# Distance attention: three square roots taken before the products

## What is computed

```
scores = einsum(q, k) / sqrt(8)
p = softmax(where(maskb, scores, -1e32)) * maskb
cum, tot = cumsum(p), sum(p)
pos = |j - i|
dist_scores = sqrt(clip((tot - cum) * pos, 0))
gamma = -softplus(gammas)              # one for each head
diff = exp(sigmoid(pdiff))             # one for each i, j
total_effect = clip(exp(dist_scores * gamma * diff), 1e-5, 1e5)
scores = softmax(where(maskb, scores * total_effect, -1e32)); row 0 set to 0
out = einsum(scores, v)
```

## Time and profile before

| | us |
|---|---|
| median of three runs | 1319.47 |
| lowest and highest | 1316.46, 1320.29 |
| the profiled execution, device time | 1316.28 |
| its span, first to last instruction | 1314.5 |
| VectorE busy, whole span | 970.5 (74%) |
| TensorE busy, whole span | 893.0 (68%) |
| ScalarE busy, whole span | 635.5 (48%) |
| layer 2, from the first product (L1301) to the last norm's copy (L189) | 88.5 to 289.2 |

### The profile page before, as it was taken

The page is one execution under the profiler, slowest core; times in us unless marked ns, Lnnn a source line. Parts: engine busy times, 40 slices in busy tenths (PEclk is TensorE's granted clock), DMA queues, the critical chain, the costliest instruction groups (busy, mean ns, idle before and its releaser), DMA issues. The chain is left out here.

```text
span 1314.5 us, 18468 instructions
## 1 busy us (share of the span) xinstructions
PE 893.0 (68%) x6150; PEld 587.3 (45%) x6150; DVE 970.5 (74%) x2494; ACT 635.5 (48%) x1392; POOL 244.2 (19%) x369
## 2 busy tenths in 40 slices
PE   5956667645887303154897938899978625999876
PEld 2523333323455103043894523576645314666644
DVE  5898989937665598987456855788868497898832
ACT  4767667631444403155214722787447421666632
POOL 1330000001000000000012211189522022332100
PEclk9975555557998656667898978899979767999978
DMA  6000000002355200010100000000000000000000
GB/s 211 2 1 0 1 1 1 1 1 96 83 105 131 45 0 34 33 67 34 33 2 1 2 1 1 0 1 1 1 1 1 1 0 0 1 1 2 1 1 16
DMA packets 26607, 30.12 MB, mean 23 GB/s; under 512 B 1169, under 2 KB 23057, under 8 KB 25490
## 3 DMA queue, kind: packets, MB, share of 16 engines
q1 hardware_dynamic: 26514, 28.95, 7.9%
HBM read 19.50 MB, written 9.44 MB: 22 GB/s over the span
## 5 line engine op out<-in xcount | busy, mean ns | idle before, releaser
L1957 PEld LDWEIGHTS l2a_b_ps<-l2a_diag,l2a_uT 128*128 128x128 f32 x512 | 66.2, 198 | 27.8 <-issue 15.4
L1957 PE MATMUL l2a_b_ps<-l2a_diag,l2a_uT 128*128 128x128 f32 x512 | 70.6, 283 | 4.8 <-DVE l2a_convh L2168 3.8
L2654 PE MATMUL l1w_mem_ps<-l1a_rows,l1w_post 128*128 128x64 f32 x16 | 4.6, 381 | 96.7 <-DVE l1a_rows L2796 96.7
L2769 DVE MATCH_REPLACE8 l1w_minus<-l1w_low,l1w_minus 128x129 f32<-128x129 f32 (+39 forms) x264 | 64.3, 256 | 0.0
L2682 ACT ACTIVATE l1w_score<-l1w_mix_ps 128x264 f32<-128x264 f32 (+7 forms) x29 | 12.0, 451 | 106.9 <-DVE l1a_rows L2796 91.1
L2763 DVE MAX8 l1w_low<-l1w_minus 128x8 f32<-128x129 f32 (+37 forms) x332 | 59.5, 254 | 0.4
L2644 PE MATMUL l1w_mix_ps<-l1a_rows,l1w_pre 128*128 128x264 f32 (+7 forms) x58 | 29.6, 681 | 42.2 <-DMA l1a_rows<-scores_dram 24.5
L2627 POOL TENSOR_SCALAR_AFFINE_SELECT l1w_score<-l1w_score 128x256 f32<-128x256 f32 x8 | 4.1, 506 | 247.5 <-ACT l1w_score L2682 247.5
L2654 PEld LDWEIGHTS l1w_mem_ps<-l1a_rows,l1w_post 128*128 128x128 f32 x16 | 4.1, 291 | 101.0 <-DVE l1a_rows L2796 99.9
L613 ACT ACTIVATE l3a_l3x_probT<-l3a_l3x_turn_ps 128x512 f32<-128x512 f32 x64 | 38.2, 596 | 22.7 <-PE l3a_l3x_turn_ps L494 22.0
L494 PE MATMUL l3a_l3x_turn_ps<-pack,l3a_l3x_prob 128*128 128x128 f32 x256 | 40.8, 282 | 10.3 <-ACT l3a_l3x_probT L613 5.7
(11 more groups left out here) (577 smaller groups left out, 2784.9 us busy)
## 6 DMA issues: line engine op xcount, KB each, us to landing
scores_dram<-l1p_dots SPq DMA_DIRECT2D x8, 924.0 KB, 7.1
l1a_rows<-scores_dram SPq DMA_DIRECT2D x5, 1056.0 KB, 4.8
l1a_rows<-scores_dram SPq DMA_DIRECT2D x24, 132.0 KB, 3.7
scores_dram<-l1p_dots SPq DMA_DIRECT2D x8, 132.0 KB, 3.8
pack<-in_pack SPq DMA_DIRECT2D x1, 761.5 KB, 9.6
pack<-in_pack SPq DMA_DIRECT2D x2, 321.5 KB, 6.6
pack<-in_pack SPq DMA_DIRECT2D x1, 612.0 KB, 11.6
pack<-in_pack SPq DMA_DIRECT2D x1, 576.0 KB, 10.6
```

Source lines behind the costliest of these rows:

```text
L1957: mm = nc.tensor.matmul(bx_ps(n)[:, j * S:(j + 1) * S], uT[:, c, b, :], diag[:, s % 2, b, :], start=True, stop=True)
L2769: nc.vector.match_replace(out=neg[:, i, 0:keys[i]], in_to_replace=low[:, i, :], in_values=neg[:, i, 0:keys[i]], imm_value=LOWEST).then_inc ...
```

## The change

In `DistanceAttention.scalar`, `root` no longer takes the root of the products: it takes the root of `left` itself, in place, as soon as the scan of that half is done. Two new steps take the root of `grid` for this batch (128 x 128) and of `rate` (128 x 16), in place, and `load_exponential_table` puts an exponential of one element behind them. `effect` now reads the products from `left` and writes `dist`. The order of ScalarE's steps in `rest()` changes as the diff shows: the roots come early, and the copies of the probabilities stand between them and the effects.

In `DistanceAttention.vector`, the products are taken out of `remaining` and become `products`, which writes back into `left`; it waits for the roots of its half, of the grid and of the rate. It stands behind `statistics`. `divide` moves behind `second_scores`. The scan waits until the effect of the batch before has read `left`, and the first step of `rate` until the products of the batch before are done.

```diff
--- before.py
+++ after.py
@@ -905,8 +905,9 @@
         self.rz = sc.sb("rz", [128, H])
         self.sums = sc.sb("sums", [128, HH, S])
         self.o, self.oT = sc.sb("o", [128, D]), sc.sb("oT", [128, D])
-        self.one_root = sc.sb("one_root", [128, 1])
+        self.one_root, self.one_weight = sc.sb("one_root", [128, 1]), sc.sb("one_weight", [128, 1])
         self.table_set = sc.sem("table_set")
+        self.grid_root, self.rate_root = sc.sem("grid_root"), sc.sem("rate_root")
         self.ln = LayerNorm(sc)
         (self.zero_set, self.ones_set, self.restart_set, self.pad_set, self.qk_mm, self.qk_set,
          self.v_mm, self.v_set, self.scores_mm, self.max_set, self.diff_set, self.first_set, self.left_set, self.rate_set, self.product_set, self.root_set, self.effect_set,
@@ -1082,11 +1083,14 @@
         last_mx = self.last_mx
         first = self.first
         dist = self.dist
+        left, rate, grid, distances = self.left, self.rate, self.grid, self.distances
+        left_set, rate_set = self.left_set, self.rate_set
+        grid_root, rate_root = self.grid_root, self.rate_root
         prob = self.prob
         probT = self.probT
         sums = self.sums
         oT = self.oT
-        one_root = self.one_root
+        one_root, one_weight = self.one_root, self.one_weight
         table_set = self.table_set
         ln = self.ln
         ones_set = self.ones_set
@@ -1116,6 +1120,7 @@
         inside = lambda b: 0 <= b < B
         turn = lambda b, half, part: 4 * b + 2 * half + part
         scale = DH ** -0.5
+        W = S + 1
 
         def first_weights(b, half):
             act.wait_ge(diff_set, 2 * b + half + 1)
@@ -1128,12 +1133,24 @@
             nc.scalar.activation(one_root[:], w("bq"), ACT.Sqrt, scale=0.0).then_inc(table_set, 1)
 
         def root(b, half):
+            act.wait_ge(left_set, 2 * b + half + 1)
+            nc.scalar.activation(left[:, half, :, 1:W], left[:, half, :, 1:W], ACT.Sqrt).then_inc(root_set, 1)
+
+        def root_grid(b):
+            act.wait_ge(distances.grid_set, b + 1)
+            nc.scalar.activation(grid[:, b, :], grid[:, b, :], ACT.Sqrt).then_inc(grid_root, 1)
+
+        def root_rate(b):
+            act.wait_ge(rate_set, 3 * b + 3)
+            nc.scalar.activation(rate[:], rate[:], ACT.Sqrt).then_inc(rate_root, 1)
+
+        def load_exponential_table():
+
+            nc.scalar.activation(one_weight[:], w("bq"), ACT.Exp, scale=0.0).then_inc(table_set, 1)
+
+        def effect(b, half):
             act.wait_ge(product_set, 2 * b + half + 1)
-            nc.scalar.activation(dist[:, half, :, :], dist[:, half, :, :], ACT.Sqrt).then_inc(root_set, 1)
-
-        def effect(b, half):
-            act.wait_ge(root_set, 2 * b + half + 1)
-            nc.scalar.activation(dist[:, half, :, :], dist[:, half, :, :], ACT.Exp,
+            nc.scalar.activation(dist[:, half, :, :], left[:, half, :, 1:W], ACT.Exp,
                                  scale=-1.0).then_inc(effect_set, 1)
 
         def exponential(b, half):
@@ -1182,18 +1199,24 @@
                     copy_v(now)
                 if inside(now):
                     load_root_table()
+                    root(now, 0)
                 if inside(now - 1):
                     copy_probT(now - 1, 0, 1)
+                if inside(now):
+                    root(now, 1)
+                    root_grid(now)
+                    root_rate(now)
+                    load_exponential_table()
+                if inside(now - 1):
                     copy_probT(now - 1, 1, 0)
+                if inside(now):
+                    effect(now, 0)
+                if inside(now - 1):
                     copy_probT(now - 1, 1, 1)
                 if inside(now):
-                    root(now, 0)
+                    effect(now, 1)
                 if inside(now - 1):
                     copy_sums(now - 1)
-                if inside(now):
-                    root(now, 1)
-                    effect(now, 0)
-                    effect(now, 1)
                 if inside(now - 2):
                     ln.act_copy(act, nc, cm, nT_ps, now - 2)
                 if now == 0:
@@ -1230,7 +1253,7 @@
         first_set = self.first_set
         left_set = self.left_set
         rate_set = self.rate_set
-        product_set = self.product_set
+        product_set, root_set, grid_root, rate_root = self.product_set, self.root_set, self.grid_root, self.rate_root
         effect_set = self.effect_set
         scaled_set = self.scaled_set
         last_max = self.last_max
@@ -1284,22 +1307,26 @@
         def remaining(b):
             for half in range(2):
                 dve.wait_ge(first_set, 2 * b + half + 1)
+                after(dve, effect_set, 2 * (b - 1) + half + 1)
                 nc.vector.tensor_tensor_scan(flat(left[:, half, :, :])[:, ::-1], flat(restart[:])[:, ::-1],
                                              flat(first[:, half, :, :])[:, ::-1], 0.0,
                                              ALU.mult, ALU.add).then_inc(left_set, 1)
             dve.wait_ge(left_set, 2 * b + 2)
+            after(dve, product_set, 2 * b)
             nc.vector.tensor_scalar(rate[:], left[:, :, :, 0], 1e-18, None, ALU.max).then_inc(rate_set, 1)
             dve.wait_ge(rate_set, 3 * b + 1)
             nc.vector.reciprocal(rate[:], rate[:]).then_inc(rate_set, 1)
             dve.wait_ge(rate_set, 3 * b + 2)
             nc.vector.tensor_tensor(every(rate), every(rate), gamma2[:], ALU.mult).then_inc(rate_set, 1)
-            dve.wait_ge(rate_set, 3 * b + 3)
-            dve.wait_ge(distances.grid_set, b + 1)
+
+        def products(b):
             for half in range(2):
-                after(dve, prob_set, 2 * (b - 1) + half + 1)
+                dve.wait_ge(root_set, 2 * b + half + 1)
+                dve.wait_ge(grid_root, b + 1)
+                dve.wait_ge(rate_root, b + 1)
                 for h in range(HALF):
                     last = nc.vector.scalar_tensor_tensor(
-                        out=dist[:, half, h, :], in0=left[:, half, h, 1:W], scalar=rate[:, half, h:h + 1],
+                        out=left[:, half, h, 1:W], in0=left[:, half, h, 1:W], scalar=rate[:, half, h:h + 1],
                         in1=grid[:, b, :], op0=ALU.mult, op1=ALU.mult)
                 last.then_inc(product_set, 1)
 
@@ -1344,14 +1371,16 @@
                     remaining(now)
                 if inside(now - 2):
                     statistics(now - 2)
+                if inside(now):
+                    products(now)
                 if inside(now + 1) and now:
                     copy_qk(now + 1)
                 if inside(now - 2):
                     ln.dve_scale(dve, nc, cm, now - 2)
+                if inside(now):
+                    second_scores(now)
                 if inside(now - 1):
                     divide(now - 1)
-                if inside(now):
-                    second_scores(now)
 
         return copy_qk, constants, differences, remaining, rest
 
```

## The result

The changed kernel takes 1303.47 us (median of 4, 1302.83 to 1304.40) against 1318.22 (median of 4) for the kernel before on the same chips: ratio 0.9893, 95% interval 0.9877 to 0.9908. That is 12.1 to 16.2 us less.

What follows compares the result with a forecast made beforehand. The prediction took layer 2 to run at VectorE's pace plus a 1.28 us gap per middle batch. Savings of 0.05 + 1.0 + 6.65 + 2.85 = 10.5 us from the 1319.47 median gave 1309.0, range 1304.5 to 1315.

Steps and rivals of the forecast that it cites:

- the effect's wait: VectorE's wait for ScalarE's effect ahead of L1311 in layer 2: 9.7 us over 8 batches, to be gone or under 1.
- A middle batch then takes 22.44 + 0.2 = 22.64: Layer 2, batches 2 to 6: VectorE's work plus a stall, 1.33 us less per batch, 6.65 for five.
- The 0.2: Ahead of the products in a middle batch: 0.1 us stall for the roots and 0.1 for added, already fulfilled waits.
- The 22.44 of VectorE work: Sum of VectorE's steps in a middle batch of layer 2, against 23.97 us with the gap and divide's wait.
- The scale: Whole time: 10.5 us less, set on the median of three runs, 1319.47, giving 1309.0 us.
- Batch 0: First batch of layer 2: early roots win what the later products lose, 0.05 us gained.
- Divide: VectorE's divide moved behind the shifts: 0.85 us less in batch 7, some 0.25 of waiting for TensorE per middle batch.
- TensorE's slack before the second difference: Middle batch: scores of the second half ready at 24.7, VectorE asks at 25.0, so 0.3 us to spare.
- the ring: Loop through scores, turned heads, copy of V, table load, roots and products; the prediction checked single waits in it.
- Rivals 1: ScalarE's table switch costs its 1.28 us twice, products stall 1.4 per middle batch: 1317.2 us in all; chance 0.04.
- rival 2: TensorE becomes the bound, its chain to the next scores 1 us later: 3.5 us lost, 1313; chance 0.09.
- 3: ScalarE's copy (0,1) between the roots is held by TensorE, products wait 4 us: 16 us slower, 1335.5; chance 0.05.

Runs made afterwards that it cites:

- no_small_roots: Changed kernel without the roots of grid and of rate, so it computes another function: 1301.13 us (1 run).
- more_waits: Changed kernel with eight more, long fulfilled waits ahead of the first product of each half: 1310.56 us, ratio 0.9958 against the kernel before.
- divide_back: Changed kernel with divide put ahead of second_scores again: 1318.52 us, ratio 1.0013 against the kernel before.
- no_early_exp: Changed kernel without the early exponential of one element, the table loading just ahead of effect 0: 1303.54 us, ratio 0.9898 against the kernel before.

## Why the prediction missed

By its own steps:

- What bounds the layer, and that the effect's wait goes: right. So were the two table loads for each batch, no drain around them (182.08 starts 0.02 after the rate's root), and the products' start in batch 1 (0.80 later than without the wait, 0.75 forecast). That the second exponentials of batch 7 come at 257.26, with 257.4 forecast, is luck: this execution came to its first scan 1.8 later than the one the forecast was built on, and the layer gave 1.9 more.
- "A middle batch then takes 22.44 + 0.2 = 22.64": this is the step that failed, as a size. It takes 22.29. The 0.2 ("Between 0 and 0.2 I take 0.1, and 0.1 more for the added waits") measured 0.09: statistics and the wait behind it take 182.20 - 181.30 = 0.90, where the sum had 0.81. Root 1 follows its scan by 0.04, and without the two small roots a middle batch is only 0.03 shorter (no_small_roots), so that next to nothing of it is a stall for the roots. more_waits doesn't show that waits in this place are free: eight more cost 0.36 there.
- The 22.44 of VectorE work was 0.24 too much. I had taken rate to the next instruction as 0.21, the step of an instruction that waits for its own engine's last result; statistics doesn't, and follows by 0.11 (181.19 to 181.30), 0.10 less. copy_qk to the norm's scaling is 0.92 (186.41 to 187.33) and not 1.02, another 0.10, and the rest is in hundredths. The 0.11 and the 0.24 are 0.35 for each of five batches, 1.75 of the 1.9 us by which the layer's sum was short.
- The scale, the other term that was mis-sized. I set the sum on the median of three, 1319.47. Later medians of the same kernel are 1316.99 (23 runs), 1317.8 (14), 1317.7 (9) and 1317.3 (9). From 1317.4 the forecast would have been 1306.9, and with the measured 12.4, 1305.0. This is 2 of the 5.5 us of the miss, the layer 1.9; what remains, 1.5, is as much as the changed kernel's own medians differ by, 1303.5 and 1304.9.
- Batch 0: -0.13, not 0.05. The products lie beside GpSimd's last steps there and take 4.63 in place of 4.29.
- Divide: the part of the mechanism that the prediction had wrong. I had it as worth 0.85 in batch 7 and, in a middle batch, the 0.25 that it waits for TensorE. divide_back shows that the early roots give nothing without its move: the layer is 15.0 longer. My own numbers had it (sums turned at r = 18.4, L1311 at 16.7), but I only asked whether divide would be late in its new place, not what its old one would cost. The sum came out near because the change had both parts, which is luck of the order and not a merit of the sum.
- TensorE's slack before the second difference, 0.3 in the prediction, was 0.57 in the trace and 0.2 for the ring. Rivals 1, 2 and 3 did not come; the ring's 0.2 says that rival 2 was close.

## What to carry to other kernels

Where an engine's wait is cut, list for each of its later instructions when its input lands, in the old order as well as in the new: two moves that are each worth nothing can be worth 12 us together. Take the step between two instructions from a row with the same pair and the same wait, since 0.1 us in a step of a loop of five is half a us. Set sums on the stretch that is changed, not on one median of three.

## What the runs showed of the hardware

- Eight fulfilled waits ahead of an instruction cost VectorE 0.35 us behind short steps, 0.06 in batch 1, where it stood idle for another engine, and nothing behind 128x128 products that were running (more_waits).
- A table load does not wait for the semaphore of the activation behind it (no_early_exp), and a switch is 1.28 us of load with 0.01 to 0.02 on each side, in all 16 of the layer, before and after. The Trainium skill's page "ScalarE: Activation LUTs", section "What ACT_TABLE_LOAD costs", adds a drain of about 1380 ns; none of these 16 has room for one.
- The same code takes up to 4.6 us more in layer 1, by TensorE's granted clock in the stretches 20 to 30 and 30 to 40 us. At 1.00 and 1.00 the first scan is at 83.3; at 0.83 and 1.00 at 84.4 to 85.2 (nine traces); at 0.66 and 1.00 at 85.8; at 0.66 or 0.67 and 0.82 or 0.83 at 87.7 to 87.9 (three).
